# Bunches of matmuls without a reader in TensorE's pauses, from the last scan to the triangle's transposes

## The reference, cut to what matters

```python
x = x + _L0_conv_ref(_gn(x), ...)      # windowed attention
x = x + _L1_conv_ref(_gn(x), ...)      # state scan
x = x + _L2_conv_ref(_gn(x), ...)      # triangle
x = x + _L3_conv_ref(_gn(x), ...)      # recurrence over rows
# end of the second, after the scan gave ys
y = (ys + u * D_param) * silu(z)
x1 = einsum('bld,ed->ble', y, out_proj_w)
x1 = (x1 - mu) * rsqrt(var + 1e-5) * gamma + beta
out = grouped_1x1(x1 * silu(grouped_1x1(x, w2)), wout)
# the third
a = sigmoid((x @ Wa1 + ba1) * (x @ Wa2 + ba2));  b = sigmoid((x @ Wb1 + bb1) * (x @ Wb2 + bb2))
g = sigmoid(x @ Wg + bg)
z = einsum('bikc,bkjc->bijc', a, b)
out = g * (_ln(z) @ Wz + bz)
```

## Time and profile before

| | us |
|---|---|
| median of 3 executions | 547.66 (546.55 to 547.82) |
| the profiled execution, its own time | 548.09 |
| its span, from the first to the last instruction | 546.6 |
| TensorE matmul busy | 387.7 (71%) |
| DVE busy | 373.4 (68%) |
| ScalarE busy | 289.5 (53%) |
| GpSimd busy | 229.6 (42%) |
| mean granted clock of TensorE | 0.874 |

### The profile page before, as it was taken

The page is one execution under the profiler, slowest core; times in us unless marked ns, Lnnn a source line. Parts: engine busy times, 40 slices in busy tenths (PEclk is TensorE's granted clock), DMA queues, the critical chain, the costliest instruction groups (busy, mean ns, idle before and its releaser), DMA issues. The chain is left out here.

```text
span 546.6 us, 10366 instructions
## 1 busy us (share of the span) xinstructions
PE 387.7 (71%) x3674; PEld 261.8 (48%) x3674; DVE 373.4 (68%) x679; ACT 289.5 (53%) x545; POOL 229.6 (42%) x205
## 2 busy tenths in 40 slices
PE   4169888899848898997995625423496181988885
PEld 3046666667635454453552201101385141987775
DVE  3797988888865003989988989974445776554443
ACT  4226888888850476837765720505476621333333
POOL 3616666777640090694795793483042000000000
PEclk9999999999997999898996755858597575999999
DMA  5100000000000000000000000000000000011111
GB/s 128 9 12 1 2 1 0 0 0 0 2 1 0 0 2 0 0 1 0 1 1 0 0 0 1 1 1 1 0 1 2 2 0 0 14 22 21 20 20 23
DMA packets 21571, 3.98 MB, mean 7 GB/s; under 512 B 19752, under 2 KB 21544, under 8 KB 21544
## 3 DMA queue, kind: packets, MB, share of 16 engines
q1 hardware_dynamic: 21416, 3.61, 4.0%
q0 software_dynamic: 128, 0.01, 0.1%
HBM read 2.00 MB, written 1.61 MB: 7 GB/s over the span
## 5 line engine op out<-in xcount | busy, mean ns | idle before, releaser
L452 POOL TENSOR_TENSOR YA<-YA,hC 128x784 f32<-128x784 f32 x28 | 53.7, 1919 | 42.2 <-DVE hC L1328 41.7
L425 POOL TENSOR_TENSOR Pr<-Pr,rc 128x392 f32<-128x392 f32 x64 | 52.3, 849 | 44.0 <-DVE rc L1263 44.0
L907 PE MATMUL pair<-BCf,sel 96*128 96x392 bf16 x128 | 39.8, 408 | 41.1 <-DVE Hs L1315 32.7
L1315 DVE TENSOR_TENSOR_SCAN Hs<-dA,pair 128x784 f32<-128x784 f32 x32 | 57.2, 1786 | 2.9 <-ACT dA L627 1.9
L921 PE MATMUL pair<-XN,BD 128*128 128x392 f32 x144 | 52.4, 513 | 5.9 <-DVE XN L1174 4.8
L907 PEld LDWEIGHTS pair<-BCf,sel 96*128 96x128 bf16 x128 | 11.0, 105 | 74.4 <-issue 71.7
L1241 DVE TENSOR_REDUCE mx<-pair 128x8 f32<-128x392 f32 x64 | 33.1, 558 | 14.0 <-PE pair L782 14.0
L570 ACT ACTIVATE PT<-pair 128x512 f32<-128x512 f32 x64 | 37.9, 592 | 7.9 <-PE pair L824 7.7
L921 PEld LDWEIGHTS pair<-XN,BD 128*128 128x128 f32 x144 | 28.0, 198 | 25.8 <-issue 9.8
L824 PE MATMUL pair<-ident,Pr 128*128 128x128 f32 x256 | 37.3, 285 | 3.5 <-POOL Pr L425 3.3
L1308 DVE TENSOR_TENSOR pair<-DU,pair 128x784 f32<-128x784 f32 x32 | 31.2, 974 | 10.6 <-PE pair L907 10.1
(11 more groups left out here) (201 smaller groups left out, 944.9 us busy)
## 6 DMA issues: line engine op xcount, KB each, us to landing
XT<-in_x SPq DMA_DIRECT2D x4, 392.0 KB, 5.7
out<-Os SPq DMA_DIRECT2D x28, 56.0 KB, 1.8
NB<-in_L_conv_x_proj_w SPq DMA_DIRECT2D x4, 3.0 KB
DW<-in_L_conv_dw SPq DMA_DIRECT2D x4, 1.1 KB
vec<-in_L_conv_b_qkv POOLq DMA_DIRECT2D x3, 0.5 KB, 6.5
W<-in_L_conv_w_qkv SPq DMA_DIRECT2D x1, 48.0 KB
BL<-in_L_conv_bi SPq DMA_DIRECT2D x3, 0.5 KB
BL<-in_L_conv_bf SPq DMA_DIRECT2D x3, 0.5 KB
```

Of the source, the lines that this page charges most:

```text
L425: eng.tensor_tensor(pg, pg, bcast(rc[:, g, :], 2, WT), ALU.mult).then_inc(pn_r, 1)
L452: eng.tensor_tensor(y, y, hC[:, n % NHC, :], ALU.add).then_inc(g_ya, 1)
L907: ins = eng.matmul(SPREAD[s][:, HT * h:HT * h + HT], sel[:, n, :], upper(BCf[:, c % 2, s, HT * h:HT * h + HT]), start=True, stop=True)
L1315: eng.tensor_tensor_scan(Hs[:, n % 2, :], dA[:, n % NA, :], SPREAD[0], 0.0, ALU.mult, ALU.add).then_inc(v_s, 1)
```

## The change

A helper `spare(n, bk)` issues n matmuls of `sel` (96 rows) with itself: 128 columns of weights, 512 columns of moving data, bf16, into a PSUM bank that nothing reads at that time. They signal nothing. Calls of it stand in TensorE's program in four places, each behind a wait for a step of the chain: 26 matmuls in step 4 ahead of the product "out" of image 3, 9 in step 5 ahead of its "wout", 10 ahead of the triangle's factors, and 14 ahead of the transposes. Nothing else is changed, and no other engine's program.

```diff
+            def spare(n, bk):
+
+                for _ in range(n):
+                    eng.matmul(banks[bk][:, :], sel[:, 0, :], sel[:, 0:4, :].rearrange("p n c -> p (n c)"), start=True, stop=True)
+
+            def spare_tail(i):
+
+                if i == J:
+                    eng.wait_ge(v_s, DS * J)
+                    for n in (3, 4, 5, 6, 7):
+                        eng.wait_ge(g_ya, (DS - 1) * (J - 1) + n)
+                        spare(5, 0)
+                    eng.wait_ge(v_y1, J)
+                    spare(1, 0)
+                if i == J + 1:
+                    eng.wait_ge(c_["var"], J)
+                    spare(4, 0)
+                    eng.wait_ge(a_rs, J)
+                    spare(2, 0)
+                    eng.wait_ge(g_nt0, J)
+                    spare(2, 0)
+                    eng.wait_ge(v_nt1, J)
+                    spare(1, 0)
+
             def pe_ssm(i):
@@
+                spare_tail(i)
                 spread("B", 0)
@@
                 pe_ssm(i)
 
 
+            eng.wait_ge(c_["wout"], J)
+            spare(4, 0)
+            eng.wait_ge(s_mv, 3)
+            spare(4, 0)
+            eng.wait_ge(s_rs, 3)
+            spare(2, 0)
             eng.wait_ge(s_xn, 3 * J)
@@
                 ins.then_inc(t_z, 1)
+            eng.wait_ge(t_zc, G)
+            eng.wait_ge(t_za, G)
+            spare(4, 6)
+            eng.wait_ge(t_v, G)
+            spare(4, 6)
+            eng.wait_ge(t_r1, 1)
+            spare(4, 6)
+            eng.wait_ge(t_r2, 1)
+            spare(2, 6)
             for q in range(14):
```

## The result

The changed kernel takes 543.66 us (median of 4, 543.48 to 544.13) against 547.11 of before (median of 4, 546.47 to 547.82): a ratio of 0.9938 with a 95% interval of 0.9921 to 0.9955. Its profiled execution took 543.54 with a span of 542.1; mean granted clock 0.892 instead of 0.874, TensorE busy 400.9 us instead of 387.7. 544.3 was forecast, with a range of 541.8 to 550.3.

A forecast was written before the change was run, and what follows sets the result against it. A chain from DVE, POOL or ScalarE to TensorE and back, paid at the granted clock, was the bound. 1.0 + 0 + 1.0 + 0.3 + 1.2 + 0.1 = 3.6 off 548.09 gave 544.5, taken as 544.3; range 541.8 to 550.3.

The forecast's parts named there:

- third part: Ten matmuls ahead of the triangle's factors: no delay, less of the factors at the low clock; 1.0 us saved (0 to 1.5).
- The price of one matmul: One added 512-column matmul on TensorE: 0.43 us at the low clock, 0.215 at the high one.
- First part: 26 matmuls ahead of out: clock rises at 365.1, out starts 0.5 late, takes 1.42 less; 0.9 to 1.0 us saved.
- Second part: 9 matmuls between var and wout of image 3: delay nothing, holding the clock left open (0 or 1.4); 0 taken.
- The cap on the third part: Factors: ScalarE's queued gate evacuation stalls TensorE 1.4 us at the high clock, so the gain is at most 1.5.
- Small products: The 128 small products from 416.27: a later clock fall saves up to 0.9 us; 0.3 taken.
- Fourth part: 14 matmuls ahead of the transposes: start 0.85 late, earlier rise; 1.15 to 2.1 us saved, -0.85 without a rise; 1.2 taken.
- the sign: Behind the transposes: the first Y starts 1 to 2 us earlier relative to the last reduction if the forecast is right.
- Recurrence: Start of the recurrence: 4.9 low us against a middle of 4.65; 0.1 us saved, with 0.75 either way.
- thrown anew: Clock rises on TensorE: each comes by chance 3.4 to 5.9 us after the work set in, middle 4.65.
- The first: Rival at all places: added matmuls do not raise the clock, out starts 4.2 late; 552.0 us, chance 0.2.
- The second rival: Rises come, but the queue eats them: first place nets 0, factors begin low; 547.2 us, chance 0.2.

The follow-up runs named there:

- 32-row run: The full change with every added matmul on 32 rows of sel instead of 96; 553.22 us, ratio 1.0103 to the kernel before.
- delayed kernel: The kernel before, without added matmuls, with two more DVE products ahead of nt of image 3; 548.02 us, ratio 1.0004.
- best version: The full change with 128-row matmuls, counts re-laid in its four places, and a fifth place ahead of the recurrence; 539.93 us, ratio 0.9865 to the kernel before.
- trimmed version: The full change with 13 instead of 14 matmuls ahead of the transposes, none behind Exp; 544.14 us, ratio 0.9940 to the kernel before.
- dense second place: The full change with 18 instead of 9 matmuls ahead of wout of image 3; 544.72 us, ratio 0.9941 to the kernel before.

## Why the prediction was right, and where it was not

The sum was 3.6 against the profiled execution, and from C to the end 3.6 is what the trace shows. That the clock would rise inside the 26 and that TensorE's links behind it would be shorter was right, and the 32-row run shows that it is the clock. That the sum came out so closely is partly luck: the third part came about in another way than forecast, and errors of 0.1 to 0.3 in the terms cancel. Step by step:

- **The price of one matmul** (0.43 low, 0.215 high): 26 in 11.27 at the low level, 4 in 1.04 at the high one with the tail of the last. Right.
- **First part, 0.9 to 1.0.** Rise forecast for 365.1 with C at 360.47, so 4.6 after C; it came 4.3 after. Out started 8.05 after C instead of 7.80, so 0.25 late (0.5 forecast), and took 1.50 less: 1.25, which is what C to F measured. Right, with the term 0.25 low.
- **Second part, 0.** Right: wout at 2.98 with 0.62 of idle ahead of it, nothing delayed. The doubt was well placed: the fall stood right at its start, and 18 matmuls in its place held it.
- **Third part, 1.0.** The number (1.11) was right, the step was wrong. It gave a part to the ten matmuls (a rise in a third of the cases) and 0.6 to a rise that starts afresh with the factors. The trace shows the ten at the high level, after a rise 0.4 behind wout, and the fall 0.15 after the factors' start. The run with the first place alone has no ten and a factors stage of 22.03, so they are worth 0.07; the run with the ten but without the first has 23.08, as before. What shows in their place, in the delayed kernel too: a rise kept its time when the work was shifted against it. The factors had 5.8 low us before because of where they started; 1.25 earlier, the rise stood at 35.0 after C instead of 38.5, and they had 3.5. That this came out as a gain of the size forecast for the ten is luck.
- **The cap on the third part**, 1.5 with a stall of 1.4 for ScalarE: with the clock high throughout the stage was 21.42, that is 1.65 shorter, and the stall 0.83. The mechanism and its place were right.
- **Small products, 0.3**: 0.46, by a fall that came 2.1 after their start rather than 0.2 ahead of it. This, too, came with the first place alone (15.98).
- **Fourth part, 1.2.** The rise was forecast 4.8 to 7.3 after V (437.5 to 440.0 with V at 432.72); it came 6.6 after. The transposes started 5.64 after V instead of 4.78, so 0.86 late (0.85 forecast). V to I: 0.93 shorter, of which 0.65 is the place's own; the rest is the gap between the first two Y, which the term includes and which closes with the first place alone as well. So the term was 0.27 too large. It gave the transposes too much: it had 3.4 low and 1.7 high, but from the first transpose to WZ it takes 3.20 low and 2.29 all high (best version); here, with the rise 0.92 into them, 2.57. From WZ to the first Y it takes 1.14 instead of 2.03. The first Y therefore starts 0.63 + 0.89 - 0.86 = 0.66 earlier after V (9.35 instead of 10.01), where 1 to 2 was named as the sign. The other sign, that the ten from V on end with a high clock, did not come either: they end at 434.84, the rise is at 435.55.
- **Recurrence, 0.1**: 0.1 to 0.2 the other way, within the 0.75 allowed.
- **What the throws are.** The prediction called each rise thrown anew, and took the middle of 3.4 to 5.9 for the chance part. In the eight profiled executions with 96 rows and the first place the rise there stands 4.05 to 4.53 after C, and in all of before, delayed and without the first a rise stands 38.5 to 38.7 after C. So within these profiled executions it is no throw: these rises keep their moment, and a stage is long or short by where it starts against them. The timed executions are not all alike in this. They have no trace, but each has its mean granted clock on record: of the 57 timed executions of before in the experiments, the nine with 0.877 took 545.6 to 546.8 us and the eight with 0.871 or 0.872 took 548.8 to 549.7. So part of the scatter goes with the clock. For the profiled executions the range was too wide, and the part of the gain that came from it could have gone the other way for another length of the stages.
- **The rivals.** The first was refuted for 96 rows in the first place, and the trace of 32 rows shows its price: 7.0, where the prediction had 3.9 net. It left the two products behind out at the high level and took back 1.2 for later rises; in the trace both ran low, which costs 2.8, and what came back in the factors and small products (0.1 and 0.5) went again in V to I (0.7). Its doubt about sel matmuls was half right: with 96 rows there was a rise in the first place and none over the 13 matmuls of the fourth, where 128 rows had one. The second rival, that the queue eats the gain, held in part in the fourth place: there the late end cost the 0.53 that the trimmed version took back. What the dense second place lost was no matter of the queue.
- **The transposes** run at the granted level: 14 instructions in 3.41 low, and eight in 1.26 high in the best version. The Trainium skill (TensorE: Matmul & The Clock Gate, Part 4: PE-mode transpose) says that the full clock does not engage for transposes; these rows, like the earlier trace rows, show otherwise.
- **Two readings of the rows.** The granted clock is not 9 tenths or more everywhere before 287 us: three earlier slices show 7, 8 and 8. And the four rises of the earlier trace rows lie in one execution, so they cannot speak for how rises differ from run to run.

What stays open: what the values of the operands do beside the rows was not tried; why a rise keeps its moment is not shown; and the mean clocks tell that timed executions differ, but not in which stage.

## What to carry to other kernels

Price a matmul link on a chain by the granted clock under it; where TensorE idles between links, unread matmuls cost nothing here as long as their queue ended before the real operand was ready. The bunches that paid here used 96 or 128 of the 128 rows; 32 rows cost 7.0, and 9 matmuls spread over 5 us did not keep the clock for a link that 18 kept it for. Do not judge a place by its own link: the first place gained 1.25 at its link and 3.1 in all, a filled second gap gained 1.4 and kept 0.2, and five filled gaps gave 8.3 from C to the end. And compare such variants by stage lengths from a common mark, not by the total: part of any gain or loss is only the place where the work now stands against the clock's changes.

## What was not expected of the hardware

- A rise kept its time when the work ahead of it moved: 38.5 after C before, 38.7 with the factors 1.76 later. Of 1.76 us of added delay 1.4 disappeared by the end.
- The rows in use count, in the one pair that differs in nothing else. 26 matmuls of 512 columns brought a rise with 96 rows (4.3 after C) and none with 32 in 11.3 us, nor in 41 busy us around them. In the fourth place 13 brought a rise with 128 rows and none with 96, but these also differ in the values that they read.
- A fall can stand within 0.2 of the start of a link, on either side (380.9 before wout at 381.0; 391.2 after the factors at 391.0; 457.2 after the input products at 457.05). In the first of these the link took 2.98 instead of 1.58.
